# Searching eigenvalues by leading minors in two rounds, and a twisted factorisation with its two directions on the two halves of the partitions

## What is computed

```python
h = relu(layernorm(x)); x = x + L0(h, adj)   # graph conv, two linear layers, two batch norms
h = relu(layernorm(x)); x = x + L1(h, adj)   # two graph convs, then LSTMs over windows of 1 to 4 nodes
h = relu(layernorm(x)); x = x + L2(h, adj)   # spectral layer
h = relu(layernorm(x)); x = x + L3(h, adj)   # three graph convs with weights adj * adj

def L2(features, A, W1, b1, W2, b2):
    deg = sum(A, 0) + sum(A, 1) - diagonal(A)
    L_norm = d_inv_sqrt[:, None] * (diag(deg) - A) * d_inv_sqrt[None, :]
    _, U = eigh(L_norm)
    agg = einsum('mn,bnd->bmd', U.T, features)
    out = relu(agg @ W1 + b1) @ W2 + b2
    return einsum('nm,bmd->bnd', U, out)
```

## Time and profile before

| what | us |
|---|---|
| median of 3 runs (1081.61 to 1082.16) | 1082.08 |
| the profiled execution, its own time | 1077.69 |
| span of that execution | 1075.9 |
| PE matmul busy | 942.6 (88%) |
| DVE busy | 593.2 (55%) |
| ACT busy | 529.3 (49%) |
| POOL busy | 335.7 (31%) |

### The profile page before, as it was taken

One profiled execution on the slowest core, in us unless ns is written; L12 is line 12 of the kernel. 1 busy time (PEld: TensorE's weight loads), 2 busy tenths in 40 slices (PEclk: granted clock), 3 DMA queues, 4 the chain that ended last, 5 costly groups with the idle time before them and its releaser, 6 DMA issues.

```text
span 1075.9 us, 12192 instructions
## 1 busy us (share of the span) xinstructions
PE 942.6 (88%) x3721; PEld 573.0 (53%) x3721; DVE 593.2 (55%) x2897; ACT 529.3 (49%) x962; POOL 335.7 (31%) x404
## 2 busy tenths in 40 slices
PE   2787485589989999899898999995899999999998
PEld 1444232544546544456344553553675865866856
DVE  5899766767634785347999198965410501503101
ACT  1566364475453654536546365441646445445531
POOL 1333100036544265441665527653210200300000
PEclk9989798699999999999998999997799999999999
DMA  7000000000000000000000000000000100100101
GB/s 309 0 2 1 0 0 1 1 0 1 0 1 1 1 0 2 1 0 1 1 0 1 0 1 1 1 1 0 1 1 0 41 1 1 40 1 1 41 0 40
DMA packets 2961, 13.26 MB, mean 12 GB/s; under 512 B 464, under 2 KB 464, under 8 KB 2640
## 3 DMA queue, kind: packets, MB, share of 16 engines
q1 hardware_dynamic: 2896, 12.49, 2.9%
HBM read 8.30 MB, written 4.19 MB: 12 GB/s over the span
## 4 chain that ended last, share of the span: by engine, by line
PE 69%; DVE 19%; POOL 5%; ACT 4%; issue 2%; DMA 0%; SPq 0%; DVEq 0%; ACTq 0%; POOLq 0%
PE PS L384 68%; POOL BIG L846 4%; DVE ST L1354 2%; ACT T L750 2%; DVE T L1450 1%; DVE stats L1326 1%; ACT BIG L788 1%; DVE sc L1043 1%; DVE PS L1112 1%; ACT BIG L780 1%; DVE vcol L1040 1%; PE PS L541 1%; POOL sc L826 1%; DVE PS L1116 1%; DVE S L1061 1%
## 5 line engine op out<-in xcount | busy, mean ns | idle before, releaser
L384 PE MATMUL PS<-BIG,wts 128*128 128x512 f32 (+2 forms) x1264 | 520.8, 569 | 19.2 <-ACT BIG L780 10.0
L384 PEld LDWEIGHTS PS<-BIG,wts 128*128 128x128 f32 x1264 | 243.5, 198 | 255.1 <-issue 206.6
L846 POOL TENSOR_TENSOR BIG<-BIG 128x256 f32<-128x256 f32 (+2 forms) x272 | 257.4, 950 | 299.6 <-ACT BIG L780 239.1
L780 ACT ACTIVATE BIG<-PS,lbias 128x256 f32<-128x256 f32 (+2 forms) x312 | 170.6, 561 | 172.5 <-PE PS L384 171.5
L688 ACT ACTIVATE BIG<-PS 128x1024 f32<-128x1024 f32 x64 | 65.5, 1023 | 88.5 <-PE PS L384 88.5
L1465 DVE TENSOR_TENSOR X<-X,PS 128x512 f32<-128x512 f32 x64 | 43.4, 682 | 118.5 <-PE PS L384 87.1
L696 ACT ACTIVATE T<-X,shift,rstd 128x128 f32<-128x128 f32 x192 | 78.4, 482 | 52.4 <-DVE shift L1342 52.4
L688 ACT ACTIVATE T<-PS 128x512 f32<-128x512 f32 x96 | 55.3, 593 | 98.1 <-PE PS L384 98.1
L384 PE MATMUL PS<-T,wts 128*128 128x512 f32 x192 | 99.4, 648 | 1.1 <-ACT T L688 0.8
L1486 DVE TENSOR_TENSOR T<-PS,wts 128x512 f32<-128x512 f32 x16 | 11.1, 691 | 150.9 <-PE PS L384 150.9
L834 POOL TENSOR_SCALAR rstd<-mv 128x4 f32<-128x4 f32 x48 | 10.9, 228 | 234.5 <-DVE mv L1333 234.5
(11 more groups left out here) (235 smaller groups left out, 1148.3 us busy)
## 6 DMA issues: line engine op xcount, KB each, us to landing
X<-x_in SPq DMA_DIRECT2D x1, 4096.0 KB, 12.5
out<-X SPq DMA_DIRECT2D x16, 256.0 KB, 2.0
wts<-w_in SPq DMA_DIRECT2D x1, 3605.5 KB, 21.3
cst<-cst_in SPq DMA_DIRECT2D x1, 371.0 KB, 3.3
AA<-adj_in SPq DMA_DIRECT2D x2, 16.0 KB, 2.0
```

Source lines behind the costliest of these rows:

```text
L384: return nc.tensor.matmul(o, l, r, start=start, stop=stop)
L780: nc.scalar.activation(LB[:, q, {"i": I_, "g": G_, "f": F_, "o": O_}[g], 0:n], PS[:, 3 * q + rank[q] % 3, 0:n], ACT.Tanh if g == "g" else ...
L846: nc.gpsimd.tensor_tensor(out, a, b, op).then_inc(pool_set[q], 1)
```

## The change

The search is done in two rounds. The first round's points are not per eigenvalue: the 128 x 32 points of all partitions (`C("spread")`) together cover the spectrum, each partition compares its 32 counts with all 64 eigenvalue numbers (`C("lanes")`), and a PE product of the result `tmp` with ones adds over the partitions. The second round is as before, 64 points for each eigenvalue.

A round has no pivots any more. It runs leading minors from both ends, `Z` [128, 65, 32], by a three-term recurrence: 31 passes of four multiply-adds, two from the top and two from the bottom, with one rescaling in the middle (ten instructions). Changes of sign are counted by a comparison of neighbours and an adding tree of six steps, in place of the reduction.

The twisted factorisation has its downward direction on partitions 0 to 63 and its upward one on 64 to 127 (`Tdir` holds the reversed coefficients). It, too, is a three-term recurrence: 64 passes of two one-element multiply-adds, with a rescaling of six instructions after 16, 32 and 48. Ratios of neighbours replace the pivots, and a new PE product with `C("fold")` ("ways") brings the two directions together; so the strand has 13 `prep` products instead of 12.

The paces become 34.0 and 26.0 for the rounds, 24.0 up to "ways" and a new 12.0 from there to "V". The diff, cut to its core:

```diff
-ROUNDS = 3
+ROUNDS = 2
-PACE_GRID = 38.0
-PACE_TWIST = 45.0
+PACE_GRID = [34.0, 26.0]
+PACE_TWIST = 24.0
+PACE_SCAN = 12.0
...
                 for n in range(ROUNDS):
-                    yield PACE_GRID
+                    yield PACE_GRID[n]
                     pe.wait_ge(grid_cnt, n + 1)
-                    mm(eb(2)[:, 0:1], C("fold"), sc[:, 3:4]).then_inc(grid_sum, 1)
+                    if n == 0:
+                        mm(eb(2)[:, 0:1], tmp[:, :], ones[:, 0:1]).then_inc(grid_sum, 1)
+                    else:
+                        mm(eb(2)[:, 0:1], C("fold"), sc[:, 3:4]).then_inc(grid_sum, 1)
 
                 yield PACE_TWIST
+                pe.wait_ge(prep_dve, PREP["ways"])
+                prep(mm(eb(0)[:, 0:P], C("fold"), both_ways[:, :]))
+                yield PACE_SCAN
                 pe.wait_ge(prep_dve, PREP["V"])
...
+                    for i in range(1, HALF):
+                        j = NODES - 1 - i
+                        up, dn = HALF - i, HALF + i
+                        gsync(1)
+                        gop(v.scalar_tensor_tensor(ta, xn, d[:, i:i + 1], Z[:, up, :], ALU.add, ALU.mult))
+                        gsync(1)
+                        gop(v.scalar_tensor_tensor(tb, xn, d[:, j:j + 1], Z[:, dn, :], ALU.add, ALU.mult))
+                        gsync(1)
+                        gop(v.scalar_tensor_tensor(Z[:, up - 1, :], Z[:, up + 1, :], ne2[:, i - 1:i], ta,
+                                                   ALU.mult, ALU.add))
+                        gsync(1)
+                        gop(v.scalar_tensor_tensor(Z[:, dn + 1, :], Z[:, dn - 1, :], ne2[:, j:j + 1], tb,
+                                                   ALU.mult, ALU.add))
+                        if i == HALF // 2:
...
-                    for i in range(HALF):
-                        gop(v.reciprocal(rq[:, 0, :], Qh[:, i, :]))
-                            gop(v.reciprocal(rq[:, 1, :], Qh[:, j, :]))
-                        gop(v.scalar_tensor_tensor(Qh[:, i + 1, :], rq[:, 0, :], ne2[:, i:i + 1], Qh[:, i + 1, :],
-                                                   ALU.mult, ALU.add))
-                            gop(v.scalar_tensor_tensor(Qh[:, j - 1, :], rq[:, 1, :], ne2[:, j - 1:j], Qh[:, j - 1, :],
-                                                       ALU.mult, ALU.add))
...
-                    gop(v.tensor_scalar(Qh[:, :, :], Qh[:, :, :], 0.0, None, ALU.is_lt))
+                    gop(v.tensor_scalar(Z[:, 0:NODES, :], Z[:, 0:NODES, :], 0.0, None, ALU.is_lt))
-                    gop(v.tensor_reduce(cnt[:, :], Qh[:, :, :].rearrange("p i m -> p m i"), AX, ALU.add))
+                    gop(v.tensor_tensor(Z[:, 0:NODES - 1, :], Z[:, 0:NODES - 1, :], Z[:, 1:NODES, :], ALU.not_equal))
+                    w = HALF
+                    while w:
+                        gop(v.tensor_tensor(cn.unsqueeze(1) if w == 1 else Z[:, 0:w, :], Z[:, 0:w, :], Z[:, w:2 * w, :],
+                                            ALU.add))
+                        w //= 2
+                    if r == 0:
+                        seen = Z[:, 0:NODES, :]
+                        gop(v.tensor_tensor(seen, cn.unsqueeze(1).broadcast_to([P, NODES, M]),
+                                            C("lanes").unsqueeze(2).broadcast_to([P, NODES, M]), ALU.is_le))
+                        gop(v.tensor_reduce(tmp[:, 0:NODES], seen, AX, ALU.add))
+                        v.tensor_copy(tmp[:, NODES:P], tmp[:, 0:NODES]).then_inc(grid_cnt, 1)
...
-                for i in range(NODES - 1):
-                    v.reciprocal(s1(14), top[:, i:i + 1]).then_inc(twist_ops, 1)
-                    v.reciprocal(s1(15), bot[:, j:j + 1]).then_inc(twist_ops, 1)
-                    v.tensor_scalar(top[:, i + 1:i + 2], s1(14), ne2[:, i:i + 1], top[:, i + 1:i + 2],
-                                    ALU.mult, ALU.add).then_inc(twist_ops, 1)
-                    v.tensor_scalar(bot[:, j - 1:j], s1(15), ne2[:, j - 1:j], bot[:, j - 1:j],
-                                    ALU.mult, ALU.add).then_inc(twist_ops, 1)
+                for i in range(NODES):
+                    s, j = divmod(i, 16)
+                    at = seg[:, s, j + 1:j + 2]
+                    if i < NODES - 1:
+                        top_op(v.tensor_scalar(t2[:, i + 1:i + 2], at, ne2d[:, i:i + 1], None, ALU.mult))
+                    top_op(v.tensor_scalar(seg[:, s, j + 2:j + 3], at, ad[:, i:i + 1], t2[:, i:i + 1] if i else 0.0,
+                                           ALU.mult, ALU.add))
+                    top_sync()
+                    if j == 15 and i < NODES - 1:
...
+                step(v.tensor_copy(both_ways[high, NODES:P], mul[high, ::-1]), "ways")
+                small_product()
+                dve.wait_ge(prep_pe, 6)
```

## The result

The changed kernel takes **1107.82 us** in the median of 4 runs (1106.63 to 1109.73), the kernel before 1082.07 on the same chip: a ratio of 1.0241, 95% interval 1.0223 to 1.0258, or 25.7 us. I had forecast 1099.0 in a range of 1085 to 1110: slower, and by more than I said.

A forecast was written before the change was run, and what follows sets the result against it. PE, kept full by L1, bounds the kernel; the strand on DVE costs only PE's waits and L1's tail. 5.8 + 0 + 10 + 4 + 2.3 + 4.3 - 9.55 = +16.9 us, from 1082.08 to 1099.0, range 1085 to 1110.

The forecast's parts named there:

- The tail behind L1: Strand steps left after L1 ends: they go, so stage D's statistics start 8.55 us earlier; with PE products, gain 9.55 us.
- A round: DVE's time for one search round: 34.4 us for the first (33 to 38), 29.8 for the second.
- the second sum: PE's product adding up round 2: PE gets there at 602.7 us, after DVE is ready at 591, so no wait.
- the overlap: DVE's short instructions start 0.09 us before the one before ends, so a multiply-add costs 0.15 us.
- Term 1, the first sum: PE's product adding up round 1: PE waits 6.7 us where it waited 0.92, net +5.8 (4.5 to 9.5).
- Term 3, "ways": PE's product joining the twist's two directions, iteration 3: PE waits 10 us (7 to 13) for DVE.
- Term 4, V and I+E: PE's products behind "ways" in iteration 3: waits of about 4 us (2 to 5) and 2.3 (1 to 3).
- Term 5, the clock: PE at half clock behind the two new waits of 6.7 and 10 us: 4.3 us lost (0 to 6).
- The rival on the other side: Slack in L1 takes PE's waits, more than 17 of 22 us vanishing; only the gain is left: 1074.5 us, chance 0.12.

The follow-up runs named there:

- e4_before_paces: The kernel before with only its paces changed (40, 28 and 38 for the three rounds, 42 up to V): 1072.63 us.
- e10_before_fill2: e4_before_paces with products nothing reads: 12 in 256-column gates of iterations 0 to 2, 30 ahead of stage D, 12 ahead of its first `BDST` product: 1068.48 us.
- e6_before_38: The kernel before with only its paces changed (38, 22 and 44 for the rounds, 38 up to V): 1079.56 us.
- e7_before_fill: e6_before_38 with products nothing reads in five PE waits unrelated to the strand, twice what fit, the gates' ones placed too early: 1098.38 us.
- e12_search_alone: The changed kernel with the twisted factorisation of the kernel before, placed 60 behind the second sum: 1085.07 us.

## Why the prediction was right, and where it was too small

Direction, places and mechanism held: PE's waits at the strand's small products are what the change costs. The sum was too small, +16.9 us where the two traces differ by 30.7 and the medians by 25.7. By its own terms:

- **The tail behind L1**: 9.55 us forecast, 9.6 measured. Right.
- **A round**: 29.8 us for the second one, 32.3 measured (562.57 to 594.85). The passes gave 1 us (0.63 for 0.60), the signs and the comparison of neighbours 1.74 and 2.67 for 1.23 and 2.3, the tree 0.6. The items that the prediction lists for it add up to 29.4 and not 29.8. The cover was wide enough: PE didn't wait at the second sum. One reading of mine was too short: the section of the Trainium skill that the prediction sets against the overlap ("VectorE: DVE Perf Modes", The DRAIN you can't avoid) also says that a next op that is not held starts earlier. So the overlap in the earlier trace rows and the 0.63 us for four multiply-adds, each 0.25 us long, don't speak against it.
- **Term 1, the first sum**: net +5.8 forecast, 11.9 measured (12.79 for 0.92), outside the 4.5 to 9.5 that I gave. DVE was ready at 561.9 and not at 558, 2 us by the later start of the round (515.45 for 513.50, which is 0.7 from the reflections and 1.2 from one more held step, more on that below) and 2 by the longer steps; and PE got there at 549.2 and not at 551.2, since iteration 2's turn waited 2.41 us for 3.75 with no half clock behind it. The wait is a difference of two times, and both missed to the same side. That the missing set-up over 2048 elements ahead of DVE's adds would also shorten the turn's wait was to be read from the earlier trace rows; I left it out.
- **Term 3, "ways"**: 10 forecast, 9.69 measured, with the pass of the twist at the forecast 0.43.
- **Term 4, V and I+E**: 4 and 2.3 forecast, 6.45 and 4.57 measured. This step failed in size, and the rows show by what. From "ways" to V DVE took 20.2 us (651.77 to 671.93) and not 16. Of that it waited 2.7 for PE, 0.96 for the "ways" product and 0.90 and 0.85 for those of `wg1`, which ran at half clock; and six instructions took 0.95 to 1.24 us beside POOL's products of 512 columns, where ten had taken 0.41 to 0.74 beside those of 256. PE got to V's place after 13.7 us and not 11.5, again at half clock. For I+E I took DVE's durations from L1's end, where POOL is idle. Moved into iteration 3, the same steps stand beside POOL's products. POOL, and DVE from the ritz step on, in the changed kernel:

```profile
690.99 2.60 POOL L857 TENSOR_TENSOR BIG<-BIG 128x512 f32<-128x512 f32 x2 [0.94 <-ACT BIG L791]
```

```profile
689.14 0.98 DVE L1322 TENSOR_TENSOR EV<-EV 64x64 f32<-64x64 f32 x1
...
691.21 1.12 DVE L1326 TENSOR_TENSOR EV<-EV 64x64 f32<-64x64 f32 x1
692.36 1.27 DVE L1327 TENSOR_SCALAR EV<-EV 64x64 f32<-64x64 f32 x1
693.67 0.22 DVE L1328 TENSOR_TENSOR EV<-EV 64x64 f32<-64x64 f32 x1
```

  Three of them take 1 to 1.3 us, where they took 0.2 before; the last two end at 692.33 and 693.63, and POOL's two products, by halves of their row, at 692.29 and 693.59. So the chain from ritz to I+E took 6.4 us for 3.6. I had cost the products that moved, but not the company that they moved into.
- **Term 5, the clock**: 4.3 forecast for two waits. There were four. Behind "ways" eight records took 5.39 us for 3.60 in the kernel before, behind V six took 4.76 for 2.96, behind I+E 26 took 13.95 where the rate of 10.54 for 24 gives 11.4; with some 2 us behind the first sum that is about 8 us (an estimate from these rows). Filling the waits gave 4 to 5 back.
- **The strand's products in their new places**: put at nothing. The sum counts them as gone from L1's end, but in iteration 3 they take 3.6 us of PE's time from `both_ways` to `EV`, by the starts of the products behind them.
- **What I had not got**: the wait for ACT in iteration 2's gates grew from 3.42 to 5.06 behind the first sum. The slack that one rival hoped for went the other way there, and inside iteration 3 it gave some 2.7 us (the three waits for POOL between 645 and 652 us of the kernel before are not in the changed one).
- **The rival on the other side** wanted more than 17 of 22 us of waits to vanish in slack. Only these 2.7 did, and 1.6 came on top.
- **From trace to median**: I laid the traces' difference onto the median, as the traced execution had been 4.4 us under it. The result shows 5 us less than the traces' difference. The next section has a possible cause.

Between the traces the sum missed 13.8 us. The terms give +6.1 for the first sum, -0.3 for "ways", +4.7 for V and I+E, about +3.8 for the clock, +3.6 for the small products and +1.6 for ACT, less 2.7 of slack and the 2.2 by which PE was ahead at iteration 2's first 336-column gate: 14.6, which is 0.8 too much; clock and slack are estimates. The medians took 5 us of the miss back and left 8.8. That part is luck: laid onto the median, as I had done it, the traces' difference would have given 1112.8, outside the range. The time lies 2 us under the upper end of the range, which was set by every term at its worst.

## What the runs showed that I had not expected

**The old search has two paths through its first steps.** In the trace of the kernel before three of DVE's short instructions ahead of round 1 are held, that is, they take about 1.2 us in place of 0.2; in the trace of e4_before_paces, whose DVE instructions up to there are the same, it is five. Kernel before, DVE:

```profile
508.43 1.18 DVE L1076 TENSOR_TENSOR Trow<-Trow 128x64 f32<-128x64 f32 x1
509.64 1.16 DVE L1077 TENSOR_SCALAR Trow<-Trow 128x64 f32<-128x64 f32 x1
...
511.61 1.23 DVE L1081 TENSOR_TENSOR Trow<-Trow 128x63 f32<-128x63 f32 x1
```

e4_before_paces, DVE, and what PE then waits:

```profile
509.52 1.32 DVE L1074 TENSOR_SCALAR Trow<-Trow 128x64 f32<-128x64 f32 x1
510.87 1.23 DVE L1076 TENSOR_TENSOR Trow<-Trow 128x64 f32<-128x64 f32 x1
...
512.87 1.23 DVE L1080 TENSOR_TENSOR Trow<-Trow 128x64 f32<-128x64 f32 x1
514.13 1.19 DVE L1081 TENSOR_TENSOR Trow<-Trow 128x63 f32<-128x63 f32 x1
...
515.99 1.29 DVE L1102 TENSOR_SCALAR xg<-cst,sc 128x32 f32<-128x32 f32 x1
```

The last of these took 0.52 us in the kernel before.

```profile
520.95 1.09 PE L541 MATMUL PS<-cst,T 128*128 128x128 f32 x4 [5.70 <-DVE X L1465]
```

The wait at iteration 2's turn is 3.75 us with three held instructions (the kernel before, e10_before_fill2) and 5.70 with five (e4_before_paces, e6_before_38, e7_before_fill); with the new search it is 1.24 with three (e12_search_alone) and 2.41 with four (the changed kernel). The kernel before was timed between 1076.7 and 1083.3 us, and its traced execution of 1077.69 lies near the lower end. That its upper times are executions with the longer path would fit, but no trace was taken of one, and one run speaks against the path as the whole cause: the traced execution of e12_search_alone, with three held, was the slowest of its five (1086.64 us). So it stays a guess.

The holding itself agrees with the Trainium skill ("SBUF — State Buffer", Who interferes with whom): DVE and GpSimd share a second pair of ports, it is an exclusive lock, and the loser waits for the whole instruction. Here 128x64 elements took 1.2 us in place of 0.2, and one of POOL's products 1.25 to 1.30.

**PE's half clock follows waits of very different length.** The turn's wait of 3.75 us brought it, 2.41 us at the same place did not. Behind filled products gaps of 2.31, 1.87 and 1.45 us did, and one of 1.56 did not. And filling is worth something only where PE sets the pace behind the wait: three gates in L1 gave 4 us, stage D's start none.

## What to carry to other kernels

When small products wait in the queue of the bound engine, their places are worth more than the arithmetic behind them: moving five numbers made the changed kernel 33 us faster, and moving three made the kernel before 7.6 faster. Before a hidden chain is shortened, look where its engine waits for its own products (15.03 us in one piece here, 23.08 before): the steps behind such a wait start that much later than they could. Hidden work isn't free either: the new twist made L1's own adds late and cost 3 to 5 us. And price a step that is moved by the engines beside which it will run, not by those beside which it ran.
